# Casting three weight blocks one after the other, and loading one expert slab in halves, in an attention plus mixture-of-experts kernel on eight cores

## The reference, cut to what matters

```python
xn = layernorm(x)                                  # x: (8, 2048, 1024) f32
# attention, 16 heads of 64, causal
qkv = xn @ w_qkv.T                                 # w_qkv (3072, 1024): q, k, v
attn = softmax(mask(q @ k.T / 8)) @ v
a = attn @ w_out.T
# mixture of experts, 4 experts, the best 2 by router logits xn @ wr + br
h_e = gelu(xn @ w1[e] + b1[e])                     # w1 (4, 1024, 4096)
y_e = h_e @ w2[e] + b2[e]                          # w2 (4, 4096, 1024)
c_e = gelu(b1[e]) @ w2[e] + b2[e]
f = sum over the 2 chosen e: gate_e * (y_e - c_e + sum of all c)
out = x + a + f
```

## Time and profile before

| | us |
|---|---|
| median of 2 runs | 3321.48 (3321.37 to 3321.6) |
| the profiled execution | 3305.21 |
| its span (slowest core, 7) | 3303.7 |
| spans of the eight cores | 3286.3 to 3303.7 |
| TensorE busy | 2827.4 (86%) |
| VectorE, ScalarE busy | 785.1 (24%), 863.6 (26%) |

### The profile page before, as it was taken

How to read it: one execution, slowest core, us unless ns; L and a number is a source line. 1 busy time by engine, 2 the same in 40 slices (tenths; PEclk the granted TensorE clock), 3 DMA queues, 4 the chain that set the end, 5 groups by cost and what they waited for, 6 DMA issues and landing times. The chain is left out here.

```text
span 3303.7 us, 30071 instructions; the slowest of 8 cores (3286.3 to 3303.7 us)
## 1 busy us (share of the span) xinstructions
PE 2827.4 (86%) x11124; PEld 1082.4 (33%) x11124; DVE 785.1 (24%) x1057; ACT 863.6 (26%) x1169; POOL 35.6 (1%) x60
## 2 busy tenths in 40 slices
PE   2469867778878885999999999999999999999970
PEld 0123311111111112444444444444444444444420
DVE  4251343322222111111111111111111121111224
ACT  2122154545545552111111111111111111111100
POOL 0000000000000000000000000000000000000000
PEclk8678956565565556999999999999999999999955
DMA  8610000000000105032033023303311330330017
GB/s 155 97 29 1 17 10 26 0 26 0 1 26 1 26 0 102 1 51 35 17 51 51 13 39 52 52 1 51 51 27 26 51 51 5 47 51 1 1 53 252
DMA packets 79693, 127.86 MB, mean 39 GB/s; under 512 B 36158, under 2 KB 36286, under 8 KB 79298
## 3 DMA queue, kind: packets, MB, share of 16 engines
q0 software_dynamic: 33600, 75.50, 15.3%
q1 hardware_dynamic: 45954, 50.44, 5.0%
HBM read 176.26 MB, written 25.17 MB: 61 GB/s over the span
## 5 line engine op out<-in xcount | busy, mean ns | idle before, releaser
L854 PE MATMUL P<-xn_fm,w1g 128*128 128x512 bf16 x4096 | 896.8, 380 | 27.0 <-PEq L43 27.0
L885 PE MATMUL P<-w2g,h_sb 128*128 128x512 bf16 x4096 | 894.3, 379 | 0.0
L862 ACT ACTIVATE h_sb<-P,b_sb 128x512 bf16<-128x512 f32 x512 | 351.8, 687 | 1445.4 <-PE P L854 1445.4
L904 DVE SCALAR_TENSOR_TENSOR accum<-P,agate,accum 128x1024 f32<-128x1024 f32 x240 | 308.1, 1284 | 1379.9 <-PE P L885 1379.9
L854 PEld LDWEIGHTS P<-xn_fm,w1g 128*128 128x128 bf16 x4096 | 400.1, 98 | 515.2 <-issue 37.1
L885 PEld LDWEIGHTS P<-w2g,h_sb 128*128 128x128 bf16 x4096 | 400.7, 98 | 483.4
L701 ACT ACTIVATE p_sb<-P,cneg 128x1024 bf16<-128x1024 f32 x320 | 353.0, 1113 | 404.4 <-PE P L693 404.1
L722 PE MATMUL P<-p_sb,v_ext 128*65 128x512 bf16 x320 | 191.2, 597 | 123.2 <-DVE p_sb L709 65.7
L729 PE MATMUL P<-p_sb,v_ext 128*65 128x512 bf16 x320 | 194.4, 607 | 0.0
L709 DVE TENSOR_TENSOR p_sb<-p_sb,masks 128x1024 bf16<-128x1024 bf16 x128 | 88.0, 691 | 407.6 <-ACT p_sb L701 407.6
L281 PE MATMUL P<-xn_fm,wqkvT 128*128 128x512 bf16 x448 | 115.8, 402 | 78.5 <-DMA wqkvT<-wqkv_bf 57.5
(11 more groups left out here) (111 smaller groups left out, 942.4 us busy)
## 6 DMA issues: line engine op xcount, KB each, us to landing
w1g<-w POOLq DMA_DIRECT2D x16, 2048.0 KB, 18.2
w2g<-w POOLq DMA_DIRECT2D x16, 2048.0 KB, 28.8
attn_sc<-proj SPq DMA_DIRECT2D x16, 512.0 KB, 2.6
xrg<-x SPq DMA_DIRECT2D x4, 2048.0 KB, 10.6
arg<-attn_sc SPq DMA_DIRECT2D x4, 2048.0 KB, 15.8
y<-outr SPq DMA_DIRECT2D x16, 512.0 KB, 2.8
xA<-x SPq DMA_DIRECT2D x3, 2048.0 KB, 25.0
wqkv_bf<-w_qkv POOLq DMA_DIRECT2D x3, 2048.0 KB, 43.2
```

What stands on the lines that cost most here:

```text
L854: t.matmul(PH67[par][:, 0:512], w1g[buf][:, dc * 1024 + hc * 128:dc * 1024 + (hc + 1) * 128], xn_fm[:, dc * 2048 + tt * 512:dc * 2048 + (t ...
L862: s.activation(h_sb[tt % 2][:, hc * 512:(hc + 1) * 512], PH67[par][:, 0:512], AF.Gelu, bias=b1_sb[:, e_ * 32 + g_ * 8 + hc:e_ * 32 + g_ * ...
L885: pt=pt, st=st, sp=sp: t.matmul(pt[:, half * 512:(half + 1) * 512], h_sb[tt % 2][:, hc * 512 + ts4 * 128:hc * 512 + (ts4 + 1) * 128], w2g[ ...
L904: v.scalar_tensor_tensor(accum[:, tsg * 1024:(tsg + 1) * 1024], pt[:, 0:1024], agate[:, tsg * 4 + e_:tsg * 4 + e_ + 1], accum[:, tsg * 102 ...
```

## The change

It does two things. POOL's second cast (Q) now waits until eight of SP's transposes (those of K) have landed, and the third (V) until sixteen have; the `w_out` cast follows the third without a wait of its own, as before. And the w1 load of the first slab becomes two DMAs on the same semaphore: the first four 128-row blocks of the slab when the pair with `i_hp == 1` of the last attention stage is through, the other four when the one with `i_hp == 3` is. The wait of `emit_h` on SW0 counts the additional DMA.

```diff
@@ -259,7 +259,11 @@
-    for g_ in (1, 0, 2):
+    for j, g_ in enumerate((1, 0, 2)):
+        if j == 1:
+            W("gpsimd", "SQT", 16 * 8)
+        elif j == 2:
+            W("gpsimd", "SQT", 16 * 16)
         I("gpsimd", "SCB%d" % g_, lambda g, g_=g_: g.dma_start(
             wqkvbf_h.ap()[g_ * 1024:(g_ + 1) * 1024, :],
             wqkv_h.ap()[g_ * 1024:(g_ + 1) * 1024, :]), 16)
@@ -810,9 +814,18 @@
+            if qt == 3 and i_hp == 1:
+                W("gpsimd", "ST", C["ST"])
+                I("gpsimd", "SW0", lambda g: g.dma_start(
+                    w1g0[:, 0:4096].rearrange("p (dc hh) -> p dc hh", hh=1024),
+                    w1_h.ap()[0, 0:512, 0:1024]
+                    .rearrange("(dc p) hh -> p dc hh", p=128)), 16)
             if qt == 3 and i_hp == 3:
                 W("gpsimd", "ST", C["ST"])
-                emit_w1_dma(0)
+                I("gpsimd", "SW0", lambda g: g.dma_start(
+                    w1g0[:, 4096:8192].rearrange("p (dc hh) -> p dc hh", hh=1024),
+                    w1_h.ap()[0, 512:1024, 0:1024]
+                    .rearrange("(dc p) hh -> p dc hh", p=128)), 16)
@@ -846,7 +859,8 @@
         if tt == 0:
-            W("tensor", "SW%d" % (i % 2), 16 * (i // 2 + 1))
+            W("tensor", "SW%d" % (i % 2),
+              16 * (i // 2 + 1) + (16 if i % 2 == 0 else 0))
```

## The result

The changed kernel takes 3281.2 us (median of 12 executions) where the kernel before takes 3321.4 (11 executions, the two shown at first among them). The ratio of the times is 0.9906, with an interval of 0.9884 to 0.9927: about 31 us less, where 48 were forecast.

What follows compares the result with a forecast made beforehand. TensorE's 54 us idle wait for K weights was taken as the bound. Spaced casts gain 48 us, w1 halves 0: 3305.2 - 48 = 3257 us profiled, 3273 from the 3321.5 median; range 3262 to 3290.

Steps and rivals of the forecast that it cites:

- The stall: Ahead of the first K projection: first transpose lands near 61 us instead of 115, TensorE's 54.0 us wait shrinks below 5.
- The next bound: Quarter 1's transposes on TensorE: they need ScalarE's normalized tile, so start at 80.2 us, 48.9 us earlier.
- Its cause: First K transpose, 63.9 us to land: it stands behind 1.9 MB of x, which crawls at 17 GB/s beside the casts.
- Q and V: Later casts and transposes: Q 101 us early, V 84, no cost; a rival making either late had 3%.
- the advice of the Trainium skill: Spaced casts, against issuing DMAs early: by that rule alone 48 - 16 = 32 us; by the rows 48.
- K at the low clock: K projections of quarter 0: four groups of some 3.6 us each at the low clock, ending at 75 us.
- The w1 slab: Slab load in halves beside attention: 0 us, bounds -2 and +2; the boundary wait stays at 27 us.
- The sum: Whole kernel: 48 us gained, 3257 us for the profiled execution, 3273 for the median.
- From there on the order of work is as before, 48 us earlier: Everything after quarter 1's start: the work keeps its order and moves 48 us earlier, provided the weights are there.
- a shorter warm stretch could as well cost 3 us: K and layer-norm stages: possible 3 us clock loss, set against a faster-clock rival (3254 us) with 3%.
- a fixed offset: Whole kernel: the profiled execution lies 16 us below the runs' median 3321.5, so the same step gives 3273.

Runs made afterwards that it cites:

- e4: Kernel before, with POOL waiting for all of x ahead of its first cast: 3308.49 us, ratio 0.9991.
- e3: Kernel before, with only the w1 slab loaded in halves, the casts together as before: 3316.22 us, ratio 1.0011.
- e1: The changed kernel once more, unaltered: 3281.75 us, ratio 0.9916.
- e2: Kernel before, with only the casts spaced, the w1 slab in one DMA: 3283.21 us, ratio 0.9919.
- e8: Changed kernel, with V's and w_out's casts issued after the K projections of quarter 2, the second run of that kernel: 3284.81 us, ratio 0.9893.
- e10: Changed kernel, with only SP's V transposes moved behind the K projections of quarter 2: 3281.98 us, ratio 0.9889.
- e9: Changed kernel, K projections of quarters 0 to 2 evicted by ScalarE, next quarter's statistics emitted behind them: 3234.7 to 3240.0 us, once 3261.2, ratio 0.9772.
- e6: Kernel before, with 46 unused VectorE multiplications ahead of quarter 1's statistics: 3333.89 us, ratio 1.0046.
- e12: Kernel before, with K projections of quarters 1 and 2 evicted by ScalarE: 3287.9 to 3292.8 us, ratio 0.9931.
- e11: Changed kernel, with K projections of quarters 1 and 2 evicted by ScalarE: 3255.0 to 3261.3 us, once 3279.3, ratio 0.9849.

## Why the prediction was right and wrong

**The stall.** Right in its place and size. On core 3 the first transpose landed at 60.4 us instead of 115 (forecast 61), TensorE's waits for `wqkvT` shrank from 57.0 to 3.1 us, and quarter 1 began at 80.85 to 83.59 us on the eight cores for a forecast of 80.2. The next bound was the normalized tile, as forecast: 8.11 us of idle time on `xnf` ahead of L446.

**Its cause.** Wrong in one link. I put the slow transpose down to the 1.9 MB of x ahead of it (five loads, not four as I wrote); e4 took the x away and the transpose took 55.4 us all the same. What fits is the turn by packets that the prediction cited from the Trainium skill ("DMA: Bandwidth & Descriptors", Queues, rings and completion order), applied to the transpose itself: 156 small packets against 217 of 25.5 KB in 50 us. Spacing the casts helps for either reason, so the sum did not suffer.

**Q and V.** Right: on core 3 the casts went out at 85.14 and 130.87 us (forecast 85 and 136) and the last transpose at 189.2; V was first used at 288.70 on core 0, at 307.32 on core 3, and no wait for a DMA stands ahead of Q or V. The two later casts took 15.4 and 18.6 us for the 24.4 that I had taken, and V's first transpose took 20.4 us beside `w_out`'s cast, about the 20 that I had charged. That the change goes against the advice of the Trainium skill ("DMA: Bandwidth & Descriptors", Rules for kernel authors) to issue a DMA early, which I weighed against it, cost nothing here.

**K at the low clock.** On core 3 K of quarter 0 ran at 1.67 us for seven matmuls, the price of 1.00, not at the 3.15 that I had taken (on cores 4 to 6 the first group alone ran mostly at the lower clock, 3.15 us on core 4); it waited for the transposes instead, and so ended near the 75 us forecast by luck (the last seven start at 71.76).

**The w1 slab.** Right: 0 us (e3), and the wait at the block's boundary stayed:

```profile
1279.36 30.50 PE L868 MATMUL P<-xn_fm,w1g 128*128 128x512 bf16 x128 [27.82 <-PEq L43]
```

**The sum, and the step that failed.** The undisturbed cores of the changed kernel end at 3247.3 us (median of 54, with e1), those of the kernel before at 3299.0 (270 cores, run beside the experiments): 51.7 us, for 48 forecast. What failed is the sentence "From there on the order of work is as before, 48 us earlier": it puts the clock behind the moved stages at nothing, and the only term for a lost clock in the prediction is "a shorter warm stretch could as well cost 3 us". I had looked at the clock only in the stages that I moved, and at its two levels there; a third value, of 0.81, in the Q and V projections behind them was no rival at all. It measured 29.1 us on the cores that had it (3276.4 against 3247.3), and as the time is that of the slowest of eight cores, one pair is enough: each of the eleven executions counted had at least one, 23 of 44 pairs in all.

The warning stood in the first table. The profiled execution of the kernel before took 3305.2 us and the two runs beside it 3321.4 and 3321.6. I carried those 16 us along as a fixed offset. Over the 39 executions with the cores' clocks on record the kernel before takes 3303 to 3309 us without a pair at 0.81 and 3317 to 3331 with one (21 and 18). That the first two runs were of the second kind follows from their times; they have no clock of their own on record. So the offset was the same effect, rarer and cheaper: the 42 cores of the kernel before that were at 0.81 end at 3317.7 us, 19 above the others, where the change makes it 29. For the profiled execution the sum is then 3305.2 - 48 - 3.7 (the rest of the undisturbed gain) + 29.1 = 3282.6, and it took 3282.2. That the median, 3281, lies as near as 8 us to the 3273 forecast is luck: the 3321.5 that I started from had a pair at 0.81 in it already, most likely, so that the forecast had paid for part of what it did not know.

**What is open.** What makes a pair fall to 0.81. Shown: it comes to both cores of a pair together; the spacing of the casts raises its rate (e2), with V's traffic or without (e8, e10); with the wait for VectorE's copies gone from quarters 0 to 2 it is down to one pair in twenty in the changed kernel (e9). Only hinted at, for counts so small: that delaying the cores of the kernel before raises it, from 21 of 156 to ten of 36 (e6), and that removing the wait from quarters 1 and 2 alone lowers it, to none of twenty pairs in the kernel before (e12) and seven in twenty in the changed one (e11). That the change does it by bringing the cores of a pair into step is the reading that fits these. The start of the K projections hung before on a transpose that landed at another time on each core, and hangs now on each core's own statistics.

The traces bear half of this out. Take TensorE's restarts behind the wait for VectorE's copies, in quarters 1 and 2, in the ten profiles of before, the change, e1 to e6, e8 and e10, and leave out pairs that were at 0.81 already. The two cores of a pair restart at most 1.83 us apart in two of 24 cases with the casts of the kernel before (before, e3, e4), and in 30 of 46 in the kernels with spaced casts: the change does bring them together. e6 adds four. Twelve of these 36 near restarts are followed by the fall, the nearest of them on cores 2 and 3 of the changed kernel (186.06 and 186.17 us); of the 40 restarts that lie 1.91 us or more apart, none is. So near restarts went with every fall of this kind, and yet two thirds of them stayed at 1.00 (cores 4 and 5 of the changed kernel restart at 186.21 and 186.24). What else it takes isn't known, and that the nearness itself is the cause is argued rather than shown. Nor does it cover e9 and e11, where the fall came behind no such wait. Why these two, which differ in quarter 0 alone, have one and seven pairs was not tried. A delay on one core of each pair alone would settle it; the program is the same on all cores, and this wasn't tried.
